# A four-stage transformer kernel: the mixer's beginning in another order and layout, and two hardware loops written out

## The chip, the cores and the metric

One core of a Trainium2 chip runs one program. The metric is the device time of an execution in microseconds, the median of some runs. Five engines work side by side, each with its own queue of instructions, in order, joined by semaphores only: TensorE (PE), VectorE (DVE), ScalarE (ACT), GpSimd (POOL) and SyncE (SP), which here only issues DMAs.

## The reference

Four sequences ("groups") of 512 tokens of width 256 go through two layers, each a token mixer and a mixture of experts, every half behind a modulated layer norm. Cut to what matters here, with the layer norm `h = layernorm(x) * (1 + c) + s` ahead of each:

```python
x = x + ga * attention(h)          # layer 0: 16 heads of 16, low-rank adapters, causal softmax
x = x + gb * experts(h)            # layer 0: 16 experts, top 2
x = x + ga * ssm_forward(h)        # layer 1: the mixer, 64 heads of 64, state 128
x = x + gb * experts(h)            # layer 1: 32 experts, top 6, and a shared one

def ssm_forward(h):
    gate, hBC, dt = split(h @ in_proj_w.T)            # 4096, 4096 + 2 * 128, 64
    hs, B, C = split(silu(conv4(hBC) + conv_b))       # causal convolution, 4 taps
    dt = softplus(dt + dt_bias)                       # one per head and token
    Adt = -exp(A_log) * dt
    A_cum = cumsum(Adt)                               # within a chunk
    L = exp(segsum(Adt))
    Y_diag = (C B^T * L) @ (hs * dt)
    states = decayed sums over chunks of B^T (exp(A_last - A_cum) * hs * dt)
    Y_off = exp(A_cum) * (C @ states)
    y = (Y_diag + Y_off + D * hs) * silu(gate)
    return (norm_w * y / rms(y)) @ out_proj_w.T
```

## The kernel before

The stages follow each other: attention, experts, mixer, experts. At a few points ("together") all engines but SP wait for each other; elsewhere they are coupled by counted semaphores. The order of instructions on each engine is written out by hand.

**Attention** (`attn_dve` L545, `attn_act` L660, `attn_pe` L719). One pass per group, in a hardware loop `e.Fori(0, GROUPS)` on DVE, ACT and PE. Its semaphore targets and addresses depend on the turn and are computed in registers. GpSimd's part is written out already. A pass begins with the norm (`norm_dve` L196: `bn_stats` L200, `bn_aggr` L204), goes through the projections and 16 heads, and ends with `tail_dve` (L283, L287).

**The mixer's beginning** (`start_pe` L1631, `start_act` L1705, `start_dve` L1783). It makes what the stream needs for all four groups: the split rows `h_hi`, `h_lo`; from the projections of B, C and dt (`project`, four products of six accumulating matmuls, banks 0 to 3) the tables `b_tok`, `c_t`, `g_mat` from B and C, and `dt_tok`, `cum_tok`, `dec_tok`, `e_tok`, `e_in` from dt. The weights for dt are laid out with the 32 even and the 32 odd heads each repeated four times over the 128 partitions, so that each product gives four equal copies, of which 32 partitions are used. The order is a pipeline over groups, with two buffers: for each `minus_abs`, softplus (Exp and Ln, each behind a load of ACT's table), `taps` (six operations on DVE), tanh, `silu`, transposes of the sums (`turn_sums`), products of B and C (`products`, L1673 and L1676), the last sums and the decays. SP stores each group's running sums (L2006).

**The stream** (`mixer_stream` L1955 on). The mixer's 32 feature tiles of a group run through a software pipeline, one tile entering with each step, five in work (`Tile`, `back` 0 to 4). A step holds the projections of x and z (L2040), transposes of `xc` (L2054), of `y_off` (L2063), the products with the decay matrix (L2068), the state products (L2081, L2089) and the output product (L2096). The first four steps of a group are written out, then, for groups 1 to 3, twelve that also carry pieces of routing; the rest, `for it in` a `Fori` from L1985, four steps a turn, is a hardware loop: 28 steps of group 0 and 16 of each of the others. On GpSimd the steps that scatter are written out.

Of the kernel before, what the change touches and what calls it, by code (L numbers as in the profile page):

```python
# [76 lines left out]
def program(nc, io, ctx, order):  # L77
# [467 lines left out]
    def attn_dve(v):  # L545
# [15 lines left out]
        with e.Fori(0, GROUPS) as b:  # L561
            v.enter(b, ATTN_MEETS, ATTN_STEPS, ONE_GROUP)
# [78 lines left out]
            v.leave(GROUPS)  # L641
# [18 lines left out]
    def attn_act(a):  # L660
        e = a.e
        hb_hi, hb_lo = mixer_rows[0]
        with e.Fori(0, GROUPS) as b:
            a.enter(b, ATTN_MEETS, 0, ONE_GROUP)
# [48 lines left out]
            a.leave(GROUPS)  # L713
# [5 lines left out]
    def attn_pe(t):  # L719
        e = t.e  # L720
        hb_hi, hb_lo = mixer_rows[0]
        with e.Fori(0, GROUPS) as b:
            t.enter(b, ATTN_MEETS, 0, ONE_GROUP)
# [95 lines left out]
            t.leave(GROUPS)  # L819
# [56 lines left out]
    def experts(layer):  # L876
# [295 lines left out]
        def dve(v):  # L1172
# [173 lines left out]
    dt_u = sb("dt_u", [P, 2, 2, SEQ], where=start)  # L1346
    dt_v = sb("dt_v", [P, 2, 2, SEQ], where=start)
    dt_t = sb("dt_t", [P, 2, 2, SEQ], where=start)
    bc = sb("bc", [P, 2, 2, SEQ], where=start)
    th_bc = sb("th_bc", [P, 2, SEQ], where=start)  # L1350
    ct_hi = sb("ct_hi", [P, NC, SSM_HEADS], F32R, where=start)
    ct_lo = sb("ct_lo", [P, NC, SSM_HEADS], F32R, where=start)
# [35 lines left out]
     g_tanh, g_cum, g_bc, g_turned, g_bc_out, g_ct, g_last, g_last_used, g_dec, g_out, g_masked) = [  # L1388
# [3 lines left out]
            "sums_turned", "bc_products", "sums_split", "last_sums", "last_sums_used", "decays", "start_out", "products_masked")]  # L1392
# [237 lines left out]

    def start_pe(e):  # L1631

        def project(b):
            e.wait_ge(p_low, KD * (b + 1))
            if b == 0:
                e.wait_ge(g_wb, 3)
            for n, w in enumerate((2, 3, 0, 1)):
                if b and n == 0:
                    e.wait_ge(g_dt, 2 * b)
                if b and n == 2:  # L1640
                    e.wait_ge(g_taps, b)
                m = 0
                for k in range(KD):
                    for l, r in ((wb_hi, h_hi), (wb_hi, h_lo), (wb_lo, h_hi)):
                        mm = e.matmul(bank[n][:, :], l[:, w, k * P:(k + 1) * P], r[:, k, b * SEQ:(b + 1) * SEQ],
                                      start=(m == 0), stop=(m == 3 * KD - 1))
                        m += 1
                mm.then_inc(g_proj, 1)

        def turn_sums(b):  # L1650
            s = b % 2
            e.wait_ge(g_cum, b + 1)
            if b:
                e.wait_ge(g_out, 3 * b)
                e.wait_ge(g_ct, b)
                e.wait_ge(g_last_used, b)
            for c in range(NC):
                cols = slice(c * P, (c + 1) * P)
                for hh in range(2):
                    hc = slice((c * 2 + hh) * FT, (c * 2 + hh + 1) * FT)  # L1660
                    e.transpose(bank[5][:, hc], dt_v[0:FT, s, hh, cols], ident[0:FT, 0:FT])
                    mm = e.transpose(bank[4][:, hc], dt_t[0:FT, s, hh, cols], ident[0:FT, 0:FT])
            mm.then_inc(g_turned, 1)

        def products(b):
            s = b % 2
            e.wait_ge(g_bc, b + 1)
            if b:
                e.wait_ge(g_out, 3 * b)
                e.wait_ge(g_masked, b)  # L1670
            for c in range(NC):
                cols = slice(c * P, (c + 1) * P)
                e.matmul(bank[7][:, cols], bc[:, s, 0, cols], bc[:, s, 1, cols], start=True, stop=True)  # L1673
            for c in range(NC - 1):
                cols = slice(c * P, (c + 1) * P)
                mm = e.transpose(bank[6][:, cols], bc[:, s, 0, cols], ident[:, :])  # L1676
            mm.then_inc(g_bc_out, 1)

        def last_sums(b):
            e.wait_ge(g_ct, b + 1)  # L1680
            e.wait_ge(g_out, 3 * b + 1)
            n = NC * SSM_HEADS
            e.matmul(bank[4][:, n:2 * n], last_r[:, :], ct_hi[:, :, :].rearrange("p c h -> p (c h)"), start=True,
                     stop=False)
            e.matmul(bank[4][:, n:2 * n], last_r[:, :], ct_lo[:, :, :].rearrange("p c h -> p (c h)"), start=False,
                     stop=True).then_inc(g_last, 1)
# [7 lines left out]
        e.wait_ge(p_full, KD * GROUPS)  # L1694
        e.wait_ge(*p_high(KD * GROUPS))
        for b in range(GROUPS):
            if b >= 1 and b + 1 < GROUPS:
                project(b + 1)
            turn_sums(b)
            products(b)  # L1700
            last_sums(b)
        for o in range(KD):
            e.matmul(bank[o][:, :], zero_b[:, :], zero_r[:, :], start=True, stop=False, skip_group_check=True)

    def start_act(e):  # L1705
# [15 lines left out]
        def projected(b):  # L1721
            s = b % 2
            if b >= 2:
                e.wait_ge(g_turned, b - 1)
                e.wait_ge(s_lb[b - 2], 16)
                e.wait_ge(g_bc_out, b - 1)
                e.wait_ge(g_out, 3 * (b - 1))
            for n in range(2):
                e.wait_ge(g_proj, 4 * b + n + 1)
                e.activation(dt_u[:, s, n, :], bank[n][:, :], ACT.Identity, bias=dtb[:, n:n + 1]).then_inc(g_dt, 1)  # L1730
            for n in range(2):
                e.wait_ge(g_proj, 4 * b + n + 3)
                e.activation(bc[:, s, n, :], bank[2 + n][:, :], ACT.Identity, bias=cw[:, FT + n, TAPS:TAPS + 1],
                             scale=cw[:, FT + n, TAPS - 1:TAPS]).then_inc(g_bias, 1)

        def softplus(b):
            s = b % 2
            e.wait_ge(g_abs, 2 * b + 1)
            e.activation(dt_v[:, s, :, :], dt_v[:, s, :, :], ACT.Exp).then_inc(g_abs, 1)
            e.wait_ge(g_abs, 2 * b + 2)  # L1740
            e.activation(dt_v[:, s, :, :], dt_v[:, s, :, :], ACT.Ln, bias=1.0).then_inc(g_log, 1)

        def tanh(b):
            e.wait_ge(g_taps, b + 1)
            if b:
                e.wait_ge(g_bc, b)
            for n in range(2):
                e.activation(th_bc[:, n, :], bc[:, b % 2, n, :], ACT.Tanh, scale=0.5).then_inc(g_tanh, 1)

        def tables(b):  # L1750
            s, n, heads = b % 2, NC * SSM_HEADS, slice(b * FT, (b + 1) * FT)
            e.wait_ge(g_turned, b + 1)
            e.activation(dt_tok[:, :, :, heads], bank[4][:, 0:n].rearrange("p (c h f) -> p c h f", c=NC, h=2),
# [21 lines left out]
        for b in range(GROUPS):  # L1775
            if b + 1 < GROUPS:
                softplus(b + 1)
# [1091 lines left out]
```

## Time and profile before

| | |
|---|---|
| median of 3 runs | 2451.97 us (2448.23 to 2458.56) |
| the profiled execution | 2432.14 us, span 2430.3 us |
| PE busy | 1979.1 us, 81% |
| DVE busy | 1706.8 us, 70% |
| ACT busy | 1465.7 us, 60% |
| GpSimd busy | 959.4 us, 39% |
| granted TensorE clock, mean | 0.906 |

The profile is of one execution; all its times are microseconds from the span's start. Busy shares are means over stages with different limits, so each stage is to be read by itself. "issue" in the chain of waits is time in which an engine waits for nothing that the profile shows.

### The profile page before, as it was taken

The page shows a single profiled execution, that of the slowest core. Times are in us where ns is not written, and L with a number is a line of the kernel's source. Part 1 is how long each engine was busy: PE and PEld are TensorE (multiplying, and loading weights), DVE is VectorE, ACT ScalarE, POOL GpSimd, SP SyncE. Part 2 cuts the span into 40 slices and gives each one's busy share as a digit, 9 for nine tenths or more (in the row PEclk, how much of TensorE's full clock was granted, in tenths as well). Part 3 has the DMA queues.
Part 4 walks back from the last instruction along what each step waited for, and adds up shares of the span by engine and source line. Part 5 has one row for each costly group of instructions (what it writes and reads, how often), then busy time and mean ns, then how long its engine had stood idle before and what let it go on. Part 6 is the DMA issues. An engine that isn't in the chain of part 4 may idle for free.

```text
span 2430.3 us, 45380 instructions
## 1 busy us (share of the span) xinstructions
PE 1979.1 (81%) x12163; PEld 1608.3 (66%) x12167; DVE 1706.8 (70%) x3894; ACT 1465.7 (60%) x3985; POOL 959.4 (39%) x1016
## 2 busy tenths in 40 slices
PE   4785858758629844899989899899999899689995
PEld 4574646646617623688878788777887788457772
DVE  5665656567414367788889988899889988564444
ACT  1462736537204334788888788878888788325551
POOL 0120302102053310245445476556665476347551
PEclk8796878979659976999999999999999999899998
DMA  4168382725923320344434455445544353646556
GB/s 126 40 188 328 121 331 70 305 95 196 396 89 105 124 79 7 133 148 144 151 109 166 138 168 163 137 140 161 166 137 164 123 179 121 183 141 180 159 154 264
DMA packets 159615, 384.60 MB, mean 158 GB/s; under 512 B 23184, under 2 KB 84752, under 8 KB 157136
## 3 DMA queue, kind: packets, MB, share of 16 engines
q1 hardware_dynamic: 144944, 342.91, 42.6%
q0 software_dynamic: 14496, 39.73, 4.4%
q8 instruction: 64, 1.05, 0.2%
q14 instruction: 111, 0.91, 0.1%
HBM read 234.86 MB, written 147.71 MB: 157 GB/s over the span
## 4 chain that ended last, share of the span: by engine, by line
PE 56%; DVE 16%; ACT 10%; issue 7%; DMA 3%; POOL 2%; PEldq 1%; SPq 1%; DVEq 1%; ACTq 1%; PEld 1%; POOLq 0%
PE bank L2040 13%; PE bank L2096 7%; ACT work L695 5%; PE bank L2068 5%; PE bank L2486 5%; PE bank L2081 3%; PE bank L2089 3%; PE bank L2054 3%; PE bank L1042 2%; PE bank L2523 2%; DVE cv L2207 2%; DVE nmax L615 2%; PE bank L1071 2%; DMA modulated_rows<-freed_rows 2%; PE bank L2063 1%
## 5 line engine op out<-in xcount | busy, mean ns | idle before, releaser
L2040 PE MATMUL bank<-h_hi,wi 128*128 128x512 f32 x1024 | 400.9, 432 | 1.1 <-ACTq L151 1.1
L2207 DVE SCALAR_TENSOR_TENSOR cv<-bank,cw,cv 128x511 f32<-128x511 f32 (+2 forms) x384 | 287.2, 748 | 68.5 <-ACT cv L2137 43.1
L2131 ACT ACTIVATE l_mat<-l_mat,cum_tok 128x128 f32<-128x128 f32 x1024 | 315.6, 429 | 0.0
L2260 POOL TENSOR_TENSOR xdec<-xdt,dec_tok 128x384 f32<-128x384 f32 x128 | 107.6, 841 | 383.5 <-DVE xdt L2197 351.0
L2275 POOL TENSOR_TENSOR yg<-yd,sgt 128x512 f32<-128x512 f32 x128 | 228.0, 1781 | 72.4 <-DVE yd L2214 72.4
L2096 PE MATMUL bank<-wo,yg 128*128 128x256 f32 x1024 | 242.4, 380 | 1.4 <-POOL yg L2275 1.4
L2040 PEld LDWEIGHTS bank<-h_hi,wi 128*128 128x128 f32 x1024 | 193.4, 189 | 61.4 <-issue 23.4
L2040 PE MATMUL bank<-h_lo,wi 128*128 128x512 f32 x512 | 202.1, 395 | 0.0
L2096 PEld LDWEIGHTS bank<-wo,yg 128*128 128x128 f32 x1024 | 184.8, 190 | 21.7 <-POOL yg L2275 1.8
L834 POOL CAST w_hi<-w_raw 128x512 fp32r<-128x512 f32 x32 | 19.6, 612 | 444.2 <-ACTq L151 303.3
L2268 POOL TENSOR_TENSOR gates<-gates,sq 128x512 f32<-128x512 f32 x128 | 163.6, 1278 | 73.6 <-ACT sq L2148 73.2
L2153 ACT ACTIVATE thx<-cv 128x512 f32<-128x512 f32 x128 | 80.7, 630 | 176.0 <-DVE cv L2207 176.0
L2122 ACT ACTIVATE y_off<-bank,e_tok 128x64 f32<-128x64 f32 x768 | 170.9, 328 | 6.9 <-PE bank L2089 6.8
L695 ACT ACTIVATE work<-bank,nmax 128x512 f32<-128x512 f32 (+3 forms) x256 | 135.3, 535 | 65.5 <-DVE nmax L615 65.5
L2233 DVE TENSOR_TENSOR outs<-l_mat,g_mat 128x1024 f32<-128x1024 f32 x128 | 157.9, 1233 | 0.1
L2595 POOL DMA_INDIRECT chosen_rows<-experts_held,experts_kept x127 | 123.1, 969 | 70.5 <-ACT experts_held L2575 55.3
L653 DVE TENSOR_TENSOR hb<-bank,pt_hi 128x512 fp32r<-128x512 f32 (+1 forms) x192 | 114.4, 599 | 47.6 <-ACT pt_hi L648 47.4
L2068 PE MATMUL bank<-outs,xdt 128*64 128x128 f32 x2048 | 142.5, 282 | 0.0
L2185 DVE SCALAR_TENSOR_TENSOR st<-st,e_in,bank 128x64 f32<-128x64 f32 x512 | 121.2, 278 | 26.6 <-DVE st L2180 11.7
L615 DVE TENSOR_REDUCE nmax<-bank 128x1 f32<-128x512 f32 (+3 forms) x256 | 117.3, 482 | 31.0 <-PE bank L772 31.0
L2143 ACT ACTIVATE l_mat<-l_mat 128x1024 f32<-128x1024 f32 x128 | 137.9, 1078 | 0.0
L2068 PEld LDWEIGHTS bank<-outs,xdt 128*64 128x64 f32 x2048 | 111.3, 138 | 21.9 <-issue 21.9
(391 smaller groups left out, 4951.0 us busy)
## 6 DMA issues: line engine op xcount, KB each, us to landing
sorted_rows<-blank SPq DMA_DIRECT2D x16, 4644.0 KB, 33.6
wi<-in_weights_split SPq DMA_DIRECT2D x128, 512.0 KB, 3.9
l_mat<-running_sums SPq DMA_DIRECT2D x128, 512.0 KB, 4.8
experts_xt<-sorted_rows SPq DMA_DIRECT2D x174, 129.0 KB, 2.3
experts_got<-chosen_rows SPq DMA_DIRECT2D x32, 512.0 KB, 9.3
wo<-out_weights_normed SPq DMA_DIRECT2D x128, 128.0 KB, 2.1
w_raw<-in_wi SPq DMA_DIRECT2D x32, 256.0 KB, 2.7
in_weights_split<-w_hi SPq DMA_DIRECT2D x32, 256.0 KB, 2.9
```

Source lines behind the costliest of these rows:

```text
L615: last = e.tensor_reduce(nmax[:, h, q:q + 1], bank[n % 3][:, col:col + P * (q + 1)], AX.X, ALU.max, negate=True)
L695: last = e.activation(pp[:, h % 2, QOFF[q]:QOFF[q] + w], bank[u][:, col:col + w], ACT.Exp, bias=nmax[:, h, q:q + 1], accum_out=ssum[:, h, ...
L2040: mm = e.matmul(dst[:, :], l, r[:, k, tok], start=(n == 0), stop=(n == 3 * KD - 1))
L2068: mm = e.matmul(PY[rows, c * P:(c + 1) * P], xdt[:, w.four, c, rows], m_mat[:, w.two, hh, c * P:(c + 1) * P], start=False, stop=(c == NC - 1),
L2096: mm = e.matmul(token_major((bank[0], bank[1]), i), yg[:, w.two, i * P:(i + 1) * P], wo[:, w.two, :], start=False, stop=w.end, skip_group_ ...
L2122: last = e.activation(y_off[:, c, rows], PO[:, c * P + hh * SSM_P:c * P + (hh + 1) * SSM_P], ACT.Identity, scale=e_tok[:, c, hh, bass.ds(w ...
L2131: last = e.activation(part, part, ACT.Relu, bias=cum_tok[:, c, hh, bass.ds(w.g, 1)], scale=-1.0)
L2143: e.activation(l_mat[:, w.four, :, :], l_mat[:, w.four, :, :], ACT.Exp, scale=-1.0).then_inc(s_l, 1)
L2207: e.scalar_tensor_tensor(out=cv[:, w.two, n:SEQ], in0=PSX[w.two][:, 0:SEQ - n], scalar=cw[:, bass.ds(w.f, 1), TAPS - 1 - n], in1=cv[:, w.t ...
L2233: v.e.tensor_tensor(m_mat[:, w.two, :, :], l_mat[:, w.four, :, :], g_mat[:, w.b, :, :].rearrange("p c l -> p (c l)").unsqueeze(1).broadcas ...
L2268: e.tensor_tensor(sq_sum[:, w.b % 2, :], sq_sum[:, w.b % 2, :], sq[:, :], ALU.add).then_inc(s_acc, 1)
L2275: e.tensor_tensor(yg[:, w.two, :], yd[:, :], sgt[:, w.four, :], ALU.mult).then_inc(s_yg, 1)
```

## The change

Three parts. The attention's loop and the loop of the stream's steps become Python loops, so that each engine's program holds every pass, with constants in place of registers. The mixer's beginning takes dt of all four groups together: group b's product is read from partitions 32b to 32b + 31 of its own copy, so that `dt_u`, `dt_v`, `dt_t` hold the four groups on four quarters of the partitions, and `minus_abs`, softplus, `sums`, the transposes and the tables `cum_tok`, `dt_tok`, `dec_tok`, `e_tok`, `e_in` are done once for all groups. B and C stay per group, with a buffer for each. The order changes: dt products of all groups first, the statistics of the rows ahead of the wait for the constants, the low half of the weights behind the second group's rows.

```diff
-        with e.Fori(0, GROUPS) as b:
-            v.enter(b, ATTN_MEETS, ATTN_STEPS, ONE_GROUP)
+        for b in range(GROUPS):
...
-            v.leave(GROUPS)
...
-                with en.e.Fori(first, FT // U) as it:
+                for it in range(first, FT // U):
                     for u in range(U):
                         run(b, it, u)
...
-    dt_u = sb("dt_u", [P, 2, 2, SEQ], where=start)
+    dt_u = sb("dt_u", [P, 2, SEQ], where=start)
...
+        def dt_part(b):
+            e.wait_ge(p_low, KD * (b + 1))
+            if b == 0:
+                e.wait_ge(g_wb, 3)
+            if b >= 2:
+                e.wait_ge(g_dt, 2 * (b - 1))
+            for hh in range(2):
+                product(bank[b % 2 * 2 + hh][:, :], 2 + hh, b).then_inc(g_dtp, 1)
+
+        def bc_part(b):
+            if b == 0:
+                e.wait_ge(p_full, KD * 3)
+                e.wait_ge(*p_high(KD * 3))
+            if b == 1:
+                e.wait_ge(g_dt, 2 * GROUPS)
+            if b >= 2:
+                e.wait_ge(g_taps, b - 1)
+            for w in range(2):
+                product(bc_banks(b)[w][:, :], w, b).then_inc(g_proj, 1)
+
+        def turned(table):
+            for c in range(NC):
+                for hh in range(2):
+                    mm = e.transpose(bank[c // 2][:, (c % 2 * 2 + hh) * P:(c % 2 * 2 + hh + 1) * P],
+                                     table[:, hh, c * P:(c + 1) * P], ident[:, :])
+            mm.then_inc(g_turned, 1)
...
         mixer_rows_pe(e, 0)
         mixer_rows_pe(e, 1)
-        project(0)
+        dt_part(0)
         mixer_rows_pe(e, 2)
-        project(1)
+        dt_part(1)
         mixer_rows_pe(e, 3)
...
-        for b in range(GROUPS):
-            if b >= 1 and b + 1 < GROUPS:
-                project(b + 1)
-            turn_sums(b)
-            products(b)
-            last_sums(b)
+        dt_part(2)
+        dt_part(3)
+        bc_part(0)
+        bc_part(1)
+        turn_sums()
+        products(0)
+        turn_dt()
+        bc_part(2)
+        products(1)
+        last_sums()
+        bc_part(3)
+        products(2)
...
+        products(3)
...
+        def dt_in(b):
+            own = slice(b * FT, (b + 1) * FT)
+            for hh in range(2):
+                e.wait_ge(g_dtp, 2 * b + hh + 1)
+                e.activation(dt_u[own, hh, :], bank[b % 2 * 2 + hh][own, :], ACT.Identity,
+                             bias=dtb[own, hh:hh + 1]).then_inc(g_dt, 1)
...
         high(0)
         high(1)
-        projected(0)
+        dt_in(0)
         high(2)
-        softplus(0)
-        projected(1)
+        dt_in(1)
         high(3)
-        for b in range(GROUPS):
-            if b + 1 < GROUPS:
-                softplus(b + 1)
-            tanh(b)
-            tables(b)
-            if b + 2 < GROUPS:
-                projected(b + 2)
+        dt_in(2)
+        dt_in(3)
+        bias(0)
+        softplus()
+        bias(1)
+        tanh(0)
+        tanh(1)
+        dt_out()
+        bc_out(0)
+        bias(2)
+        bc_out(1)
+        tanh(2)
+        exponents()
+        bias(3)
+        tanh(3)
+        bc_out(2)
+        bc_out(3)
...
     def start_dve(v):
         e = v.e
-        v.own.add(e.memset(taken[:, 0, :], 0.0))
-        e.wait_ge(s_ssm, SSM_IN)
         for i in range(NT):
             v.own.add(e.bn_stats(stats[:, i, :], x[:, i, :]))
+        v.own.add(e.memset(taken[:, 0, :], 0.0))
...
         rows(0)
         rows(1)
+        weights()
         full(0)
         rows(2)
         full(1)
         rows(3)
-        minus_abs(0)
-        taps(0)
         full(2)
         full(3)
-        sums(0)
-        for b in range(GROUPS):
-            if b + 1 < GROUPS:
-                minus_abs(b + 1)
-                taps(b + 1)
-            silu(b)
-            tables(b)
-            if b + 1 < GROUPS:
-                sums(b + 1)
-            decays(b)
+        minus_abs()
+        taps(0)
+        sums()
+        taps(1)
+        silu(0)
+        sums_out()
+        silu(1)
+        masked(0)
+        taps(2)
+        masked(1)
+        decays()
+        silu(2)
+        taps(3)
+        masked(2)
+        silu(3)
+        masked(3)
...
         for b in range(GROUPS):
-            e.wait_ge(g_cum, b + 1)
+            e.wait_ge(g_cum, 1)
             e.dma_start(sums_kept[b * FT:(b + 1) * FT, :],
-                        dt_v[0:FT, b % 2, :, :].rearrange("p h t -> p (h t)")).then_inc(s_lb[b], 16)
+                        dt_v[b * FT:(b + 1) * FT, :, :].rearrange("p h t -> p (h t)")).then_inc(s_lb[b], 16)
```

`sums_out` copies the turned sums of all groups to `cum_tok` (two copies of 512), splits them (`ct_hi`, `ct_lo`, 1024 wide each); `exponents` is the four Exp of all groups (two of 256, two of 768).

## Rows read from the trace of the kernel before

**Rows 1.** Busy time of PE, PEld, DVE, ACT, POOL (instructions); clock, DMA share, GB/s.
```profile
980.30:2083.00 1102.70, 1044.38 (x7157) 867.81 (x7161) 968.76 (x1880) 901.11 (x2480) 616.82 (x615) 0.98 0.46 146
```
**Rows 2.** The chain that ended last, whole execution: start, length, what.
```profile
341.06 6.17 issue
349.16 3.79 issue
...
630.94 5.33 DVE stats L1175 x16
```
**Rows 3.** Who waited for whom on DVE, 190 to 500: total, times, longest.
```profile
DVE stats L200 <- issue: 18.7, 3, 6.5
...
DVE mv L204 <- issue: 10.9, 3, 3.8
```
**Rows 4.** The same chain in the stream, at the output products.
```profile
1015.16 1.73 PE bank L2096 x8
...
1232.72 1.73 PE bank L2096 x8
...
1264.02 1.74 PE bank L2096 x8
```
**Rows 5.** The chain inside one looped (1202) and one written-out step (1251).
```profile
1202.22 1.38 PE bank L2040 x6
...
1203.63 0.63 PE bank L2054 x4
...
1251.48 0.44 PE bank L2054 x4
```
**Rows 6.** Busy time of four written-out steps and of looped ones with scattering.
```profile
1240.40:1263.80 23.40, 23.40 (x167) 20.07 (x166) 21.55 (x40) 20.65 (x59) 11.81 (x10) 1.00 0.35 109
1380.20:1508.90 128.70, 128.26 (x883) 105.97 (x882) 112.68 (x208) 108.24 (x304) 87.94 (x105) 1.00 0.54 166
```
**Rows 7.** Timeline at the seam between attention's second and third group.
```profile
343.83 1.28 ACT L243 ACT_TABLE_LOAD   x1 [12.22 <-issue]
```
**Rows 8.** The page's DMA queues: packets, MB, share of 16 engines.
```profile
q8 instruction: 64, 1.05, 0.2%
```
**Rows 9.** The chain in the mixer's beginning, 860 to 1016.
```profile
871.51 5.34 DVE stats L1788 x16
...
880.81 1.39 DVE xn L1807 x4
...
888.63 8.02 PE bank L1645 x24
...
978.17 0.46 DVE g_mat L1872
...
980.34 1.62 PE bank L2040 x6
```
**Rows 10.** The same chain in one cycle of the loop over groups.
```profile
942.89 1.16 ACT th_bc L1748 x2
...
945.42 2.08 PE bank L1673 x8
...
948.18 0.69 DVE g_mat L1872
948.87 1.14 DVE dt_t L1845
...
950.95 2.34 DVE dt_v L1851 x2
...
954.35 1.16 ACT dt_u L1730 x2
955.51 1.34 ACT bc L1733 x2
...
959.17 1.06 ACT dt_v L1741
```
**Rows 11.** Groups by form in 864.7 to 980.3: the convolution's taps.
```profile
L1833 DVE SCALAR_TENSOR_TENSOR bc<-bank,cw,bc 128x511 f32<-128x511 f32 x8 | 5.6, 744 | 1.8 <-ACT bc L1733 1.6
```

More of the change, by code:

```diff
@@ L662, in attn_act @@
         hb_hi, hb_lo = mixer_rows[0]
-        with e.Fori(0, GROUPS) as b:
-            a.enter(b, ATTN_MEETS, 0, ONE_GROUP)
+        for b in range(GROUPS):
             def effective_high():
@@ L721, in attn_pe @@
         hb_hi, hb_lo = mixer_rows[0]
-        with e.Fori(0, GROUPS) as b:
-            t.enter(b, ATTN_MEETS, 0, ONE_GROUP)
+        for b in range(GROUPS):
             e.wait_ge(w_b, b + 1)
@@ L818, in attn_pe @@
             t.together()
-            t.leave(GROUPS)
     def attn_pool(g):
@@ L1629, in mixer_rows_pe, with bc_banks, product @@
         mm.then_inc(p_turned.sem, 1)
+    DT_OUT, B_OUT, E_IN_OUT = 1, (2, 4, 7, 9), 6
+    def bc_banks(b):
+        return (bank[4], bank[5]) if b % 2 == 0 else (bank[2], bank[3])
     def start_pe(e):
-        def project(b):
+        def product(dst, w, b):
+            m = 0
+            for k in range(KD):
+                at = slice(k * P, (k + 1) * P)
+                for l, r in ((wb_hi, h_hi), (wb_hi, h_lo), (wb_lo, h_hi)):
+                    mm = e.matmul(dst, l[:, w, at], r[:, k, b * SEQ:(b + 1) * SEQ], start=(m == 0),
+                                  stop=(m == 3 * KD - 1), skip_group_check=True)
+                    m += 1
+            return mm
+        def dt_part(b):
             e.wait_ge(p_low, KD * (b + 1))
@@ L1636, in project @@
                 e.wait_ge(g_wb, 3)
[L1637 to L1648, printed above, removed]
@@ L1657, in turn_sums, with products @@
+        def products(b):
+            e.wait_ge(g_bc, b + 1)
+            if b:
+                e.wait_ge(g_out, B_OUT[b - 1])
+                e.wait_ge(g_masked, b)
+            else:
+                e.wait_ge(p_full, KD * GROUPS)
+                e.wait_ge(*p_high(KD * GROUPS))
             for c in range(NC):
                 cols = slice(c * P, (c + 1) * P)
[L1659 to L1673, printed above, removed]
+                e.matmul(bank[7][:, cols], bc[:, b, 0, cols], bc[:, b, 1, cols], start=True, stop=True)
@@ L1719, in high @@
                              bias=shift, scale=scale).then_inc(p_high.sem, 1)
[L1721 to L1741, printed above, removed]
+        def dt_in(b):
[4 more added lines that the diff above has]
+                             bias=dtb[own, hh:hh + 1]).then_inc(g_dt, 1)
@@ new lines, in bias, with softplus @@
+        def bias(b):
+            for w in range(2):
+                e.wait_ge(g_proj, 2 * b + w + 1)
+                e.activation(bc[:, b, w, :], bc_banks(b)[w][:, :], ACT.Identity, bias=cw[:, FT + w, TAPS:TAPS + 1],
+                             scale=cw[:, FT + w, TAPS - 1:TAPS]).then_inc(g_bias, 1)
+        def softplus():
+            e.wait_ge(g_abs, 1)
+            e.activation(dt_v[:, :, :], dt_v[:, :, :], ACT.Exp).then_inc(g_abs, 1)
+            e.wait_ge(g_abs, 2)
+            e.activation(dt_v[:, :, :], dt_v[:, :, :], ACT.Ln, bias=1.0).then_inc(g_log, 1)
@@ L1743, in tanh @@
         def tanh(b):
             e.wait_ge(g_taps, b + 1)
[L1745 to L1753, printed above, removed]
-                         ACT.Copy, scale=0.5).then_inc(g_out, 1)
+            if b >= 2:
+                e.wait_ge(g_bc, b - 1)
@@ L1755, in tables, with dt_out, bc_out @@
+            for w in range(2):
+                e.activation(th_bc[:, b % 2, w, :], bc[:, b, w, :], ACT.Tanh, scale=0.5).then_inc(g_tanh, 1)
+        def dt_out():
+            e.wait_ge(g_turned, 2)
+            for o in range(2):
+                last = e.activation(dt_tok[:, 2 * o:2 * o + 2, :, :].rearrange("p c h f -> p (c h f)"), bank[o][:, :],
+                                    ACT.Copy, scale=0.5)
+            last.then_inc(g_out, 1)
+        def bc_out(b):
             e.wait_ge(g_bc_out, b + 1)
```

143 lines of the change are left out of this document (71 added, 72 removed).

## The prediction

> **What bounds the kernel now.** I read three views: busy time by stage, then the chain of waits of the whole execution, then the chain and the timeline inside the three places that the edit touches.
>
> The stage view shows that no single engine bounds everything. In the mixer's stream (980.3 to 2083.0) TensorE is busy 1044 of 1102.7 us [rows 1]. Before it, from DVE's arrival at 864.7, lies the mixer's beginning, 115.6 us in which the chain jumps between DVE, ACT and TensorE.
>
> In the attention loop the reader is to look at the seam between two groups. DVE is through with one group at 341.06, and for 6.17 us the next one's first `bn_stats` doesn't start; after four of them it stands still for 3.79 us more [rows 2]. The chain calls both "issue": no semaphore that the profile knows is late. The same pair stands at all three back-edges: DVE's waits before L200 sum to 18.7 us in 3 times, those before L204 to 10.9 us in 3 [rows 3]. After the fourth group, where the loop is left instead of taken again, DVE's next `bn_stats` (L1175, the next stage) starts at 630.94 [rows 2], 0.2 us behind its last addition. So the stall belongs to the jump back, not to the work or its data.
>
> In the stream the chain meets the eight output products of each tile (L2096) once a step. From 1015.16 to 1232.72 lie 27 steps of the `Fori` loop: 8.058 us each. From 1232.72 to 1264.02 lie four steps that are written out already (the first four of the next group): 7.825 us each [rows 4]. The work is the same. Inside the step the six products before take 1.38 us; the transposes of `xc` (L2054) then stand for 0.63 us in the looped step and for 0.44 us in the written-out one [rows 5]. In the loop TensorE's own queue computes a register for a wait and a load address; written out, the numbers are constants and the queue runs ahead. In the groups with routing, 16 looped steps take 128.7 us, 8.04 each, with TensorE busy 128.26 of it [rows 6].
>
> **The change part by part.**
>
> *Attention written out.* ACT, DVE and TensorE lose the jump, its registers and the fetch behind it. 18.7 + 10.9 = 29.6 us, less what straight code needs there (0.2 us before `bn_stats`, as at 630.94, and as little before L204), three times: 28.5 us. What is late next? ACT must load a table before the square root; it does so at 343.83 for 1.28 us [rows 7], itself only after its own jump. In straight code it starts as DVE does, and is done before DVE has its variance (four `bn_stats` and the rest, about 2.3 us). So nothing takes the stall's place. Inside the group I take nothing: DVE's and ACT's register operations stand between instructions that wait for each other anyway. Bounds: 18 us if one of the two fetches stays (18.7 less 0.6), 31 if the inner waits shrink too.
>
> TensorE has to fetch in every group what it now keeps. The page counts 64 instruction packets of 1.05 MB on its queue, 16 KB each [rows 8], and none of the chain's pieces in written-out code is such a fetch: I cost it at nothing, covered by running ahead, and price the opposite below.
>
> A rule of the Trainium skill (Runtime: NRT & Kernel Launch, "Instruction fetch mechanics") says that fetching is sequential and mostly hidden in straight code, and that a taken branch to a page outside the window stalls until it is fetched. By that rule alone the trace agrees at the attention's seams, and the stream, whose loop body TensorE can hold, would gain nothing from being written out: the sum would then be 60 us instead of 77. The rows of the stream say otherwise, by the register work and not by the jump.
>
> *Stream written out.* 28 steps of the first group and 16 of each of the other three are looped, 76 in all. First group: 27 x (8.058 - 7.825) = 6.3 us, with the 28th 6.5. The others: 3 x (128.7 - 16 x 7.825) = 3 x 3.5 = 10.5. Sum 17.0 us. SP loses its register moves as well; its DMAs stay the same in number and size. Beside TensorE lies DVE with 21.55 us busy of 23.4 in written-out steps [rows 6], so there is cover, but a thin one. Bounds: 0 if another engine or fetching sets 8.05, 18 if all 76 gain 0.235.
>
> *The mixer's beginning.* The x-rows' statistics no longer wait for the constants' DMAs: `bn_stats` moves from 871.51 [rows 9] to DVE's arrival, 864.8. The statistics end at 871.6 instead of 878.4, but ACT still waits for the DMAs (871.51), then runs `wb_hi` (1.06, as wide as the Exp of [rows 10]), a tiny exponential (0.1) and a table load (1.28) until 873.95. Square root 0.2 and DVE's five small steps 1.1: the rows start at 875.3 instead of 880.81 [rows 9]. The low weights and three small operations, 1.4 us, now come behind the second rows and hold the first `full` up by 0.8. So TensorE starts its first product at 883.9 instead of 888.63: 24 products took 8.02 us there [rows 9], the first twelve about 5.2 at the low clock and the last twelve 2.8 (0.23 each, as six in 1.38).
>
> From there, dt first: four parts of twelve products, 5.2 + 3 x 2.8, between them the transposes of the rows (1.0 each) and waits for GpSimd's low halves of groups 2 and 3, some 1.5 in sum: 900.8. ACT's last `dt_in` 0.7: 901.5. The dt arithmetic is no cheaper per instruction, as time goes by the row of 512 and not by the partitions, but it is done once instead of four times. The pieces of a cycle of before are in [rows 10]: Exp and Ln 1.06 each, tanh 1.16, products and transposes of B and C 2.75 until the mask at 948.18, mask 0.69, dt 1.14 and 0.9, two scans 2.34, `dt_u` 1.16, bias 1.34. The taps are six of 0.744 with two small waits, 4.3 [rows 11].
>
> The new chain, with the names of the new order: bias(0) needs its products (903.5) and ends at 904.3; softplus is 1.28 + 1.06 + 1.28 + 1.06 = 4.7: 909.0 (taps(0) fits beside it). sums: 1.14 + 0.9 + 2.34 = 4.4: 913.4. taps(1) 4.3: 917.7. silu(0) 1.3: 919.0. sums_out is two copies, a wide cast and a wide subtraction, by width from 0.69 for 512 and 1.14 for 1024 about 3.6: 922.6. silu(1) and the mask 2.0: 924.6. bias(2) waits for TensorE, which did products(0), turn_dt and bc_part(2): 927.3. taps(2) 4.3, mask 0.7, decays 1.1: 933.4. ACT's exponents, not seen at this width, 2.6 by the same rule, then bias(3) 1.3: 937.3. taps(3) 4.3, tanh(3) 1.2, silu(3) 1.3, products(3) 2.7, mask 0.7: 947.5. Before, the last mask began at 978.17 and ended at 978.9, and the stream's first product began at 980.34 [rows 9]. So 31.4 us less, and the stream begins at about 949. The four stores of the sums now come at once, some 35 us before anyone reads them; SP has nothing else then. Bounds: 22 us (one more microsecond at each of the nine places where this chain changes engine), 35 us (DVE alone, never waiting from the sums on).
>
> **Sum.** 28.5 + 17.0 + 31.3 = 77 us. The profiled execution took 2432.1 us around a span of 2430.3; 2355 after. The median of the runs shown is 2452.0, that is 19.8 above the profiled one, and I keep this distance: 2375 us.
>
> **The rivals.**
>
> *The stream keeps its 8.05 us.* DVE's in-order chain through ACT (tanh, cv) or a DMA becomes the pace in a long straight run. For it: only five written-out steps in a row are seen clean, DVE is at 92% in them. Against it: in those TensorE is busy 23.4 of 23.4 us [rows 6], not waiting. 2392 us; 0.12.
>
> *The beginning gives half.* The new order puts bias(2) and bias(3) behind other work of ACT, and the taps behind them; if each round waits another 4 us, the gain is 15. 2391 us; 0.12.
>
> *The stall at the seams stays in part.* DMA engines are full there, and a prefetch may be as late as the fetch after a jump was. For it: a seam's two stalls have nothing else as cause than fetching. Against it: 630.94, equally loaded, has none. With 10 us back and the heads as they are, 2385 to 2403; 0.08.
>
> *More than forecast.* Attention's heads lose a register operation per wait: 64 heads at 0.1 to 0.2 us, 2366 us; 0.03.
>
> *Slower: straight code starves TensorE.* About 52 more blocks of instructions have to come (34 in the stream, 18 in attention). If each cost what a fetch costs after a jump, half of 6.17 us, that is +160 and 2535 us; it decides from 1.5 us per block on. Against it: the four written-out steps of [rows 4], some 115 TensorE instructions each, cross such blocks without a gap. 0.03. A further 0.02 I leave for no change at all, by some part that holds the end up.
>
> **How the numbers follow.** The forecast has 0.60. The range takes in both halves-of-gain rivals and the lower part of the third, and on the other side the upper bounds of attention and the beginning: 2364 to 2402. Within 0.5% (12 us) is what a measurement of this kernel can't tell from no change. Faster 0.95, same 0.02, slower 0.03.
>
> **What would show it.** Right: DVE's "issue" waits before L200 and L204 vanish; steps of the stream all near 7.83; dt work (`dt_v`, Exp, Ln) once and not four times; the stream begins some 60 us earlier (31 + 28.5). Wrong: "issue" gaps in TensorE at even distances (fetches), DVE or ACT as the releaser before L2054, long waits of the taps for bias in the beginning.

## The result, and the profile after

The changed kernel takes 2381.4 us (median of 4 runs, 2378.4 to 2381.6), the kernel before 2454.2 us in the same comparison: ratio 0.970, interval 0.968 to 0.973. The forecast was 2375 us, in a range of 2364 to 2402. The profiled execution after took 2381.6 us around a span of 2379.8. So it lies at the median of its runs, while that of before lay 20 us under its own; the difference of the two profiled spans is 50.5 us, that of the medians 72.7. Both the 20 us and the terms of the sum have to be accounted for.

**Attention.** The seam in the chain of waits, which answers to [rows 2]; columns are start, length, what:

```profile
332.19 1.44 DVE x L287 x4
333.64 0.02 issue
333.66 1.42 DVE stats L200 x4
...
335.21 0.39 DVE mv L204 x4
...
606.58 5.34 DVE stats L1169 x16
```

DVE goes from its last addition to the next group's `bn_stats` in 0.02 us, and on to `bn_aggr` in 0.1. The 6.17 and the 3.79 us of [rows 2] are gone, at every seam: DVE's waits of this stage (57 to 607) have no "issue" on L200 or L204 any more. The stage ends 24.4 us earlier (630.94 to 606.58).

**The mixer's beginning**, same view, which answers to [rows 9, 10]:

```profile
843.08 4.22 DMA keep<-in_keep
...
851.16 1.38 DVE xn L1833 x4
...
859.47 4.46 PE bank L1637 x12
...
878.56 0.78 ACT bc L1753
...
886.29 2.34 DVE dt_v L1881 x2
888.63 1.31 DVE bc L1864 x2
...
902.09 0.79 ACT bc L1753
...
919.23 2.08 PE bank L1697 x8
...
923.21 2.91 PE bank L2077 x6
```

Read it against the keep table's issue, at 867.21 before and 843.08 now. The two scans of `dt_v` stand once and not four times. The stream's first product comes 80.1 us behind that DMA; before it was 113.1 (980.34 less 867.21). That is 33.0 us less.

**The stream** at its output products, which answers to [rows 4], and one step of it, which answers to [rows 6]:

```profile
961.42 1.73 PE bank L2133 x8
...
1203.97 1.74 PE bank L2133 x8
```

```profile
1159.15:1166.98 7.83, 7.83 (x57) 6.72 (x56) 7.17 (x14) 6.91 (x21) 3.91 (x3) 1.00 0.46 151
```

31 steps take 242.55 us, 7.82 each, with TensorE busy all the time in the step shown. (The window of four written-out steps in [rows 6] is 23.4 us long and holds three of them, which changes nothing in its reading.) Yet the stretches around them got longer. The windows of the changed kernel: filling (first product to first output product), from there to the last output product, and from there to the end; columns as in [rows 1]:

```profile
923.21:961.26 38.05, 30.71 (x157) 24.64 (x158) 28.27 (x49) 25.29 (x64) 7.56 (x7) 0.81 0.43 146
961.26:2013.93 1052.67, 1010.29 (x6996) 858.13 (x6994) 947.66 (x1832) 883.08 (x2413) 602.77 (x603) 0.98 0.45 149
2013.93:2379.77 365.84, 293.79 (x1438) 219.19 (x1438) 182.59 (x726) 147.82 (x429) 163.54 (x210) 0.90 0.57 178
```

and two of the same stretches before:

```profile
980.34:1015.00 34.66, 26.32 (x156) 20.83 (x157) 26.55 (x47) 24.32 (x63) 6.45 (x6) 0.95 0.45 160
2079.49:2430.34 350.85, 289.54 (x1438) 216.23 (x1438) 182.25 (x726) 147.99 (x429) 163.96 (x210) 0.93 0.60 185
```

The filling is 3.4 us longer, at a granted clock of 0.81 instead of 0.95. The last stage, which nobody edited, is 15.0 us longer. Of the stream's forecast 17 us only 8.4 arrive (first product to last output product, 1099.1 to 1090.7).

Where the rest of it is lost the windows show. From the 39th output product to the 40th (a step with routing in the second group), and two pieces of that step, after:

```profile
1273.44:1285.48 12.04, 9.52 (x57) 7.96 (x56) 11.24 (x30) 7.26 (x20) 5.28 (x4) 0.86 0.31 100
1277.40:1279.40 2.00, 0.17 (x1) 0.20 (x2) 1.86 (x8) 2.00 (x3) 0.00 (x0) 0.91 0.50 199
1279.40:1281.40 2.00, 2.00 (x13) 1.67 (x14) 1.86 (x3) 0.07 (x1) 0.28 (x1) 0.50 0.14 18
```

and before:

```profile
1332.66:1343.20 10.54, 8.02 (x57) 6.63 (x56) 10.19 (x29) 6.93 (x20) 4.02 (x4) 1.00 0.34 112
1336.60:1338.60 2.00, 0.14 (x2) 0.17 (x2) 1.86 (x9) 2.00 (x3) 0.00 (x0) 1.00 0.58 223
1338.60:1340.60 2.00, 2.00 (x24) 1.66 (x24) 2.00 (x3) 0.11 (x1) 0.47 (x1) 1.00 0.00 0
```

TensorE waits for DVE in both, some 2.5 us. Before, it comes back at the clock 1.00 (2.4 GHz) and does 24 products in 2 us; after, at 0.50 (1.2 GHz) and does 13. The same 57 products take 9.52 instead of 8.02 us. Four steps lose 1.5 us in this way (two each in the second and third group), none in the fourth.

### The profile page after: what moved, and what is told of

The parts are those of the page before. It is cut to its first block, busy times and chain, and to the rows that moved or that the text cites. A ratio compares the mean times of both kernels' runs of the same rounds, so it can differ in the third digit from the quotient of the medians.

```text
span 2379.8 us, 40957 instructions
## 1 busy us (share of the span) xinstructions
PE 1981.6 (83%) x12115; PEld 1624.2 (68%) x12115; DVE 1693.0 (71%) x3866; ACT 1460.2 (61%) x3963; POOL 954.2 (40%) x1016
## 4 chain that ended last, share of the span: by engine, by line
PE 54%; DVE 18%; ACT 13%; issue 6%; POOL 2%; DMA 2%; PEldq 1%; DVEq 1%; SPq 1%; ACTq 1%; PEld 1%; POOLq 0%; another core or an unknown queue 0%
PE bank L2077 11%; PE bank L2133 6%; ACT work L692 5%; PE bank L2105 4%; PE bank L2523 4%; DVE cv L2244 3%; PE bank L2126 3%; PE bank L2118 3%; PE bank L1036 2%; PE bank L2560 2%; ACT l_mat L2168 2%; PE bank L2091 2%; DVE nmax L614 2%; PE bank L1065 2%; PE bank L750 1%
## 5 line engine op out<-in xcount | busy, mean ns | idle before, releaser
L2077 PEld LDWEIGHTS bank<-h_hi,wi 128*128 128x128 f32 x1024 | 196.0, 191 | 62.6 <-issue 24.1
L651 DVE TENSOR_TENSOR hb<-bank,pt_hi 128x512 fp32r<-128x512 f32 (+1 forms) x192 | 114.3, 599 | 50.3 <-ACT pt_hi L646 50.1
```

Of the source, the lines that this page charges most:

```text
L2077: mm = e.matmul(dst[:, :], l, r[:, k, tok], start=(n == 0), stop=(n == 3 * KD - 1))
```

## The experiments

Twelve kernels were timed in three comparisons, four in each. Each comparison ran on a chip of its own, beside the kernel before, which took 2430.8, 2449.5 and 2448.3 us (medians) in them. Stage lengths are from profiles, one for each kernel; ratios are from the timed runs.

**One part at a time, onto the kernel before.** The first comparison, with the kernel before itself (its edit: none).

> The kernel before, once more, nothing edited. The first profiled execution had a span of 2430.3 us, 20 us under the median of its other runs (2452), while the profiled execution of the kernel after (2381.6) lies at its own median. Theory A (a pause that comes in most executions): the profiled execution of before happened to miss a pause of 12 to 20 us in its last stage, as the one that the kernel after shows at 2119.8 to 2140; then this profile has a span of 2445 to 2455 with such a pause in it, last mixer step to end 380 to 390 instead of 368.6. Theory B (the profiled execution of before is always quicker than its other runs): span 2430 again, 368.6 again. Ratio to before 1.000 either way; its interval is what this measurement can tell.

Ratio 1.000 (0.998 to 1.002). Its last stage is 348.6 us long, its span 2435.4, close to the medians of this comparison (2430.8 and 2434.4 in two sets of runs), in which no run is near 2452. (The 368.6 and 380 to 390 of the expectation count from 18 us earlier than this window.) So there is no pause, and the profile agrees with its own runs: neither theory as I had put it, and the question went into the third comparison.

Attention's loop written out, in `attn_dve`, `attn_act` and `attn_pe`:

```diff
-        with e.Fori(0, GROUPS) as b:
-            v.enter(b, ATTN_MEETS, ATTN_STEPS, ONE_GROUP)
+        for b in range(GROUPS):
...
-            v.leave(GROUPS)
```

> The kernel before with the attention loop alone written out (DVE, ACT, TensorE). If the two traces' difference at the end of attention (630.94 to 606.58) is all of it and is kept to the end: -24.4, ratio 0.990. My prediction's term was -28.5 (0.9884). If something else of the change brought part of it, or if the later stages give it back: less than -20. Next stage's first bn_stats (line 1175 of before) at 606 to 607.

Ratio 0.990 (0.988 to 0.992). The stage ends at 606.96. So the -24.4 us are this edit's, and the ratio is in line with their being kept to the end. (Beside the kernel before of this comparison, whose stage ends at 634.66, they are 27.7: the looped stage itself varies, as told at the end.) From there to the stream's first product it takes 349.4 us, as the kernel before does. Attention:

```profile
58.22:606.96 548.74, 419.96 (x2464) 343.73 (x2464) 357.22 (x817) 294.15 (x832) 90.59 (x97) 0.85 0.55 203
```

The stream's loop written out, in `mixer_stream`:

```diff
-                with en.e.Fori(first, FT // U) as it:
+                for it in range(first, FT // U):
```

> The kernel before with the stream's loop alone written out. Predicted term -17.0 (76 steps of 8.058 to 7.825). The two traces gave only -7.9 from the stream's first product to its last step, because the filling (+3.4), the steps between groups (+0.8, +1.2) and the steps k = 38, 42, 70 and 74 (+1.5 each) got longer while the 75 others got 0.23 shorter. Theory A (fetching: the written-out code moves the instructions of these steps to other fetch borders or makes them come late): the loss appears here too, -8 to -12, ratio 0.995 to 0.9965. Theory B (the loss is due to the new order in the mixer's beginning or to that stage's buffers): -17 here, ratio 0.993.

Ratio 0.991 (0.989 to 0.994). The filling takes 34.39 us, the rest 1046.96, together 1081.35: 17.8 us less than before, and no routed step is longer than before. Theory A falls: the same written-out code loses nothing behind the old beginning.

```profile
980.96:1015.35 34.39, 26.33 (x157) 20.82 (x158) 26.68 (x47) 24.43 (x63) 6.36 (x6) 0.95 0.46 161
1015.35:2062.31 1046.96, 1001.78 (x6993) 851.84 (x6994) 949.02 (x1834) 882.76 (x2415) 603.81 (x604) 0.99 0.45 149
```

Two things in these traces bear on where the 0.23 us of a looped step come from. The 27 looped steps of the first group of before take 8.03 to 8.09 us each; a turn of the loop has four steps, so a cost of the jump would stand in every fourth step alone, and it doesn't. And from 1075 to 1250, inside the looped steps of before, no block of instructions is fetched for TensorE; with the loop written out, the same window has eleven (the line below, of the view of the DMA queues: number, MB, share), and every step is 7.82 or 7.83 us long:

```profile
q8 instruction: 11, 0.18, 0.4%
```

So a looped step's price is neither the jump nor a fetch, and in straight code the fetches cost the stream nothing. That it is the register work is what remains; no run changed that alone.

The mixer's beginning alone: the kernel after with both loops as `Fori` again (the two diffs above, reversed).

> The mixer's beginning alone changed (dt on four quarters, tables at once, new order), both loops still Fori. Predicted term -31.3; the traces gave -33.0 from the keep DMA to the stream's first product. Theory A (the stages are additive): -33, ratio 0.9865, and the filling of the stream keeps 34.7 us. Theory B (the filling got 3.4 longer because the four tables and stores come close together with the stream's first loads): filling 38 here as well, -29.6, ratio 0.988.

Ratio 0.984 (0.982 to 0.987). From attention's end to the stream's first product 314.8 us, against 349.4 to 352.6 in the two profiles of before: the whole of the gain, here -34.6 to -37.8. The filling is 35.9 us at a clock of 0.87, between the two expectations, and in the second group (not in the third) the two routed steps take 12.09 and 11.44 us. None of the five profiles with the old beginning has a longer filling or routed step. So it is behind the new beginning that this comes up, though less of it than in the changed kernel, and it shows in the clock.

**The whole, and parts taken back.** The second comparison.

> The kernel after once more, nothing edited. Attention alone, stream alone and beginning alone gave ratios 0.990, 0.991 and 0.984 beside a kernel before of 2430.8 us; their sum is -85 us, while the change as a whole gave 0.970 (-73) in its first comparison. Theory A (additive but for TensorE's clock: with the new beginning the stream's filling and the routed steps k = 38, 42, 70 and 74 run partly at the lower clock, +3.4 and four times +1.5): 0.967 to 0.970, with the pause at 2120 to 2140 of its first profile gone from the last stage (350 instead of 366 from last mixer step to end). Theory B (the pause belongs to this code, an instruction fetch at that place): the pause is there again at the same instructions, last stage 365.

Ratio 0.972 (0.969 to 0.975). The pause is there again, last stage 369.9 us; taken alone this spoke for theory B. Filling and routed steps are as in the first profile to 0.1 us (38.11, 12.04).

The stream's loop as `Fori` again in the kernel after:

> The kernel after with the stream's loop as Fori again, so that the stream's writing out is undone alone. Additive: slower than the kernel after by the 18 to 21 us that the stream alone gave to the kernel before, ratio to before 0.976 to 0.978. If writing out is worth less behind the new beginning, because the quicker code meets more of the lower clock: 8 to 10 us, ratio 0.972 to 0.974.

Ratio 0.980 (0.977 to 0.983), 21 us more than the kernel after in the medians. The profile puts only 9.5 of them into the stream: first product to last output product 1100.3 us, with the filling at 35.9 and all routed steps at 10.5 and 9.9. This kernel has the new beginning and, other than the one with the beginning alone, no routed step at the lower clock: the new beginning by itself doesn't settle on which steps it falls. The intervals of the two kernels leave 4 to 36 us between them, so the timing doesn't tell 9.5 from 21, and the profile speaks for the smaller gain.

**TensorE's clock.** Products of zeros, added to the output sums, keep TensorE busy while it waits; nothing else is changed. They go in front of the transposes of chosen tiles (`mixer_pe_step`), and, for the start, 13 of them in front of `products(3)`:

```diff
+            for _ in range(WARM.get(w.g, 0)):
+                e.matmul(bank[0][:, :], zero_b[:, :], zero_r[:, :], start=False, stop=False, ...)
             e.wait_ge(s_xc, done(w.g))
             e.wait_ge(s_st, done(w.g - 1, 3))
```

> The kernel after with 51 added products of zeros (128x128 zeros by 128x512 zeros, added to the output sums), 10 before the transposes of tiles 42, 74 and 106 and 7 before those of tiles 46, 78 and 110, where TensorE stands idle for 2.5 and 1.9 us. Theory A (the +1.5 us of the steps k = 38, 42, 70, 74 are TensorE's clock at half after that idle stretch; the profile shows 0.86 in these steps instead of 1.00): with TensorE busy there the clock stays at 1.00, steps 10.5 and 9.9 in all three groups, -6 us beside the kernel after. Theory B (fetching of instructions or a transfer is late there, and the clock only follows): steps stay at 12.0 and 11.5, or get longer by the added products.

The steps are 10.54 and 9.91 us in all three groups, at a clock of 1.00. But the filling was 35.66 us here, though no instruction ahead of it differs from the kernel after: the clock took another course from the start, so this run by itself doesn't show that the added products did it. The time is 2380.3 us, ratio 0.972 (0.969 to 0.975), beside 2382.6 and 0.972 of the kernel after: no difference.

> The kernel after with 33 added products of zeros where TensorE waits around the stream's start: 13 before the last group's B and C products (6.0 us of waiting there), 12 before the transposes of tile 1 (3.7 us) and 8 before those of tile 3 (2.3 us). Theory A (the filling is 38.0 instead of 34.7 us because TensorE comes to it at the lower clock, 0.50 until some 5 us into the stream, while before it had 9 us of products of its own just ahead): clock 1.00 at the stream's first product, filling 34 to 35.5, the last products of B and C 1.4 instead of 2.7 us; -4 to -5 us in sum. Theory B (the filling waits for DMAs or DVE): filling 38, nothing gained.

The filling takes 34.42 us (clock 0.95). The window of 2 us from the stream's first product on:

```profile
924.28:926.28 2.00, 2.00 (x9) 1.65 (x10) 0.00 (x0) 0.34 (x1) 0.00 (x0) 1.00 0.50 129
```

The 2 us before it are at 1.00 too. In the kernel after both are at 0.50; the second reads:

```profile
923.20:925.20 2.00, 1.99 (x5) 1.61 (x6) 0.00 (x0) 0.00 (x0) 0.00 (x0) 0.50 0.42 137
```

Theory A holds for the start: 3.7 us of filling come back, and the last products of B and C go from 2.08 to 1.16 us. The routed steps, left alone, are at 12.04 and 11.47 again, though TensorE enters the stream at 1.00 here. So it isn't the entry at the lower clock that brings the lower clock on them. The time is 2385.3 us, ratio 0.974 (0.971 to 0.977), so it shows no gain either.

The third comparison has both sets of zeros:

> The kernel after with both sets of added products of zeros (84 in all). Each did alone what TensorE's clock should do: filling 34.4 instead of 38.1 us, routed steps 10.54 and 9.91 instead of 12.04 and 11.47. Theory A (the two effects add): first product of the stream to its last output step 1084 to 1086 us instead of 1090.8, -5 to -7 us beside the kernel after, ratio to it 0.997 to 0.998. Theory B (a stretch kept busy in one place moves the lower clock to another, as at the borders between the groups, 19.65 instead of 19.22 in the run with the routed steps alone): 1087 or more.

First product to last output product 1083.1 us, 7.6 less than in the kernel after. This run and the one before it differ by the 51 products in the routed steps alone, and come to them alike (34.42 and 34.41 of filling), so these products do remove the lower clock there. The step is then, without and with them (the nine more matmuls in the window are of the ten zeros):

```profile
1270.89:1282.93 12.04, 9.52 (x57) 7.96 (x56) 11.24 (x30) 7.28 (x20) 5.28 (x4) 0.86 0.35 100
1271.01:1281.57 10.56, 10.14 (x66) 7.53 (x66) 10.20 (x29) 6.96 (x20) 4.04 (x4) 1.00 0.37 114
```

In the timed runs the 7.6 us don't show: 2383.7 us against 2385.7, both ratios 0.974 (0.971 to 0.976). No better version could be proved here.

**The statistics behind the constants again**, in `start_dve` of the kernel after:

```diff
         e = v.e
+        e.wait_ge(s_ssm, SSM_IN)
         for i in range(NT):
```

> The kernel after, with DVE waiting for the eight constants' DMAs in front of its 16 bn_stats again. The prediction's step: the statistics start at DVE's arrival and not when the keep table lands, and the rows 5.5 us earlier. Undone: rows begin 4.5 to 6 us later behind the keep DMA's issue, and the stream's first product comes 5 to 6 us later, as nothing else is late enough to hide it; ratio 0.002 above the kernel after. Rival: the rows' products wait for something else (GpSimd's low halves), and only 0 to 2 us come back.

```profile
842.87 3.78 DMA keep<-in_keep
...
854.95 1.38 DVE xn L1834 x4
```

```profile
927.36:963.09 35.73, 27.88 (x157) 21.92 (x157) 26.68 (x47) 24.44 (x63) 6.35 (x6) 0.91 0.45 155
963.09:2010.13 1047.04, 1001.88 (x6993) 851.86 (x6994) 949.34 (x1834) 882.80 (x2415) 603.87 (x604) 0.99 0.45 149
```

The rows begin 12.1 us behind the keep DMA's issue instead of 8.1, and the first product 84.5 instead of 80.1: +4.4 us, a little under what I expected. But the stream behind it is 8.0 us shorter: a filling of 35.7 and no routed step at the lower clock. That this is the delay's doing isn't shown: the kernel with zeros in the routed steps had a filling of 35.7 as well, with nothing edited ahead of it, and the one with the stream's loop as `Fori` again had 35.9 and no routed step at the lower clock. The ratio is 0.975 (0.973 to 0.977), no different from 0.974.

**The last stage.** The third comparison again.

> The kernel before once more, to be profiled beside the kernel after on one chip. So far: where the kernel before took 2431 us, no profile (of four kernels) has a pause in the last stage (348 to 354 us from last mixer step to end); where it took 2449 to 2454, the profiles of five kernels, all made from the kernel after, have one of 13 to 20 us (365 to 370). Theory A (the pause belongs to the chip it runs on, and both kernels have it there): if the kernel before takes 2445 or more in this comparison its profile shows 364 or more for the last stage; if it takes 2431, 348 to 352, and the kernel after 350 as well. Theory B (the pause belongs to the code of the kernel after): 350 here whatever the time, and 366 in the kernel after.

> The kernel after for the third time, beside the kernel before of the same call. Theory A (chip): last stage as long as that of the kernel before in this call, within 3 us; 2362 to 2367 us and ratio 0.972 to 0.974 on a chip without the pause, 2380 and 0.971 on one with it. Theory B (code): 366 against 350.

The kernel before took 2448.3 us in this comparison, and its last stage 369.6 us, with the pause. Here are the 20 us from 109 to 129 us behind the last output product, first in this profile, then in that of the kernel before in the first comparison:

```profile
2186.00:2206.00 20.00, 7.86 (x25) 5.38 (x25) 3.05 (x15) 3.24 (x10) 12.71 (x14) 0.64 0.34 106
2196.00:2216.00 20.00, 19.23 (x108) 15.40 (x106) 9.42 (x48) 11.87 (x36) 15.29 (x16) 1.00 0.59 181
```

The kernel after: 372.8 us, 3.2 more than the kernel before, and a ratio of 0.974 (0.971 to 0.976). Theory B falls, as the kernel before has the pause too. In the comparison where the kernel before takes 2431, all four profiles lack the pause (348 to 354 us); in those where it takes 2448 or more, all nine profiles of before, after and its variants have it (365 to 373). That speaks for theory A. One profile stands apart: the first one of the kernel before lacks the pause (350.8), though the runs beside it take 2448 to 2459. It is an execution of 2432.1 us and none of these runs, and on which chip it ran isn't known. Chip and hour aren't told apart either.

What the pause is stays open. In the kernel after, the chain has long "issue" waits of DVE there (4.33 us at 2121.57, 9.10 at 2129.44), and the window of the longer one reads:

```profile
2129.44:2138.54 9.10, 3.50 (x9) 2.29 (x9) 0.00 (x1) 0.63 (x2) 5.82 (x7) 0.50 0.33 114
```

DVE, ACT and TensorE mostly wait; GpSimd does not, but issues a scattering DMA every 1.27 us. The pause begins where these follow each other without a gap, seven or eight in 10 us. I didn't try to move that.

## Why the prediction was right, and where not

**The seams (28.5 forecast, 24.4 measured).** The mechanism held: both stalls went, at all three seams, and nothing took their place; no table load stands in the chain before the square root. The term was mis-sized at "Inside the group I take nothing". DVE waits there a little longer in written-out code. Its waits from 58 to 607, after:

```profile
DVE hb L651 <- ACT pt_hi L646: 50.1, 124, 0.7
DVE nmax L614 <- PE bank L767: 32.3, 63, 2.2
DVE h L607 <- ACTq L151: 22.9, 4, 6.1
...
DVE hb L635 <- ACT hb L707: 11.6, 4, 2.9
```

Before, the same four were 47.4, 31.0, 21.6 and 9.9: 7.0 us more now, of which some is bought back elsewhere. Of the four only the first is clear of the spread between profiles: 47.1 to 47.4 us in the five with the loop, 50.1 to 50.5 in the nine without. Why it grew isn't settled. TensorE's queue now takes 106 blocks of instructions in the page, against 64 [rows 8]: 42 more, where the forecast took some 52. In the stream they cost nothing; whether they cost something in attention, the runs don't show.

**The stream (17.0 forecast, 8.4 measured; 17.8 when it alone is changed).** The step's price was right to 0.01 us: 7.83. By the rule of the Trainium skill that I weighed against it (Runtime: NRT & Kernel Launch, "Instruction fetch mechanics") the stream would have gained nothing, as fetching was all that the rule prices. The trace agrees with it in that no block is fetched in the looped steps; the measured 17.8 us are another cost, and register work is what is left for it. What failed is what the sum left out: I priced the 76 looped steps and took all else in the stream as unchanged. The last 10 us ahead of the stream's first product, before and after:

```profile
970.34:980.34 10.00, 5.43 (x30) 4.83 (x32) 5.14 (x10) 3.88 (x11) 0.00 (x0) 0.58 0.06 15
```

```profile
913.21:923.21 10.00, 2.72 (x12) 2.35 (x12) 5.96 (x9) 2.84 (x6) 0.00 (x0) 0.67 0.00 0
```

The old order had 5.4 us of products there, and the granted clock was 1.00 from 979 on. The new one has a wait of 6.0 us and then 2.7 us of products, and TensorE enters the stream at 0.50. In the stream the lower clock falls on other steps: against the kernel with the stream alone +3.7 in the filling, four times +1.5 in routed steps and +2.3 at two borders between groups, less 2.6 in the two steps behind routed ones: the 9.4 us that are missing (1090.7 less 1081.35), to 0.1. The zeros bring 7.6 of them back, 3.7 at the start and 3.9 in the routed steps and around them. So the loss is the clock's. The 3.7 lie in the filling and go with how TensorE comes to it and waits in it (two of the three sets of zeros there stand inside the filling). Why the routed steps meet the lower clock stays open, since they do so after an entry at 1.00 too. The granted clock stands in every window of [rows 6] as 1.00, and I read it as a property of the stream.

**The beginning (31.3 forecast, 33.0 measured).** Shifted by the 24.1 us by which the keep DMA is earlier, the forecast's marks lie beside the measured ones thus: rows 851.2 and 851.16; first product 859.8 and 859.47; end of bias(0) 880.2 and 879.34; end of the sums 889.3 and 888.63; end of bias(2) 903.2 and 902.88; stream 924.9 and 923.21. The rows begin 8.1 instead of 13.6 us behind the keep DMA's issue: 5.5 as forecast, 4.0 by the statistics (their undoing showed 12.1); the other 1.5 I put to the low weights, which no run changed alone.

**The distance of 19.8 us.** I kept it without a cause, and that it came out right is luck. The profiled execution of before lacks the pause in the last stage (350.8 us, where one beside a time of 2448 has 369.6); that the runs beside it had the pause follows from their times alone. If so, the 20 us stand in the median before and after alike. The profile after has them inside (365.8), and its difference to the profile before is too small by 15 us.

**The rivals.** Straight code doesn't starve TensorE: 31 steps of 7.82 us without a gap. The seams keep nothing. The beginning gives all. The stream doesn't keep its 8.05 us; but its net gain is half, by a mechanism that no rival named. The range's lower end was set too low for its own reasons: the upper bounds of attention (31) and of the beginning (35) take 6 us off 2375, which is 2369 and not 2364.

The sum from the profiles, attention 24.4, beginning 33.0, stream 8.4, is 66 us; the medians say 73, 67 and 63 in three comparisons. My 77 was 6 to 23% above these, and the comparison that stood beside the forecast is the one nearest to it. That the time came within 7 us of 2375 is in part luck: two of the three terms were too large, by 4.1 and 8.6 us, and in the other two comparisons the same sum would have missed by 10 and 14 us.

## What to carry to other kernels

A loop's price is read at its seams and in its steps separately: the same kernel shows the step both looped and written out, and the difference times the count was right to 5%. When an edit changes what lies ahead of a stage bound by TensorE, look at the clock at which TensorE enters it, from the windows just before and after the border, and leave room for more: of the 9.4 us lost here 3.7 came in the filling, and the rest on steps 280 us and more behind it, which an entry at the full clock did not save. And compare a profile's span with the runs beside it stage by stage before using the difference: 20 us here were a pause in a stage that nobody had touched.

## What the runs showed of the hardware that I had not expected

- The lower clock in routed steps doesn't depend on the step alone. TensorE is idle for the same 2.5 us in each; the step takes 10.54 us at 1.00 or 12.04 at 0.86. Three executions of the kernel after agree to 0.1 us in this, though they reach the stream at 923.0, 923.2 and 929.2. The kernel whose statistics wait for the constants, 4 us later, has none of it (1082.8 us instead of 1090.7 from first product to last output product); one profile, so not shown to be the delay's doing. The Trainium skill (TensorE: Matmul & The Clock Gate, "What's actually happening") says that the throttled state is the default and activity releases it; the added zeros agree.
- The stall at a loop's jump is the same each time: in the five profiles with `Fori` DVE stands still for 5.7 to 6.6 us ahead of the next group's first `bn_stats`, at all 15 seams, and not more than 0.04 us in the nine without. What varies in the looped kernel lies inside the groups: attention took 566.8 to 576.2 us with `Fori`, 547.6 to 549.9 without.
- One and the same kernel has a last stage of 348.6 us in one comparison and of 369.6 in another, on different chips, each in line with the timed runs beside it; both with the same instructions, and 0.4 us apart in the stream (1099.5 and 1099.2 us).
